# One gap of pad rows after routing, an earlier load for the second head unit, and shared weights loaded inside attention

## The reference, cut to what matters

```python
q, k, v = jnp.split(x @ W_attn.T + b_attn, 3, axis=-1)          # heads: 16 x 16
att = softmax(where(causal, q @ k.T / 4 + rel_bias, -inf))
x = layernorm(x + (att @ v) @ W_proj.T + b_proj)
top1 = argmax(softmax(xf @ gate_w.T))                            # one of two experts
masked = xf[None] * one_hot(top1)                                # the other expert sees zeros
expert_out = relu(masked @ w1 + b1) @ w2 + b2                    # both experts, summed
shared = relu(xf @ sw1 + sb1) @ sw2 + sb2
x = layernorm(x + expert_out.sum(0) + shared)
```

## Time and profile before

| | us |
|---|---|
| median of three executions | 850.62 (843.71 to 852.77) |
| profiled execution, its own time | 847.82 |
| its span in the profile | 846.1 |
| projection, to the first scores of attention | 101.5 |
| attention, 16 units | 101.5 to about 402 |
| PE busy, of the span | 787.3 |
| ACT busy | 547.4 |
| DVE busy | 507.0 |
| POOL busy | 235.2 |

### The profile page before, as it was taken

One profiled execution on the slowest core, in us unless ns is written; L12 is line 12 of the kernel. 1 busy time (PEld: TensorE's weight loads), 2 busy tenths in 40 slices (PEclk: granted clock), 3 DMA queues, 4 the chain that ended last, 5 costly groups with the idle time before them and its releaser, 6 DMA issues.

```text
span 846.1 us, 15471 instructions
## 1 busy us (share of the span) xinstructions
PE 787.3 (93%) x5805; PEld 561.3 (66%) x5805; DVE 507.0 (60%) x1102; ACT 547.4 (65%) x700; POOL 235.2 (28%) x194
## 2 busy tenths in 40 slices
PE   6999879999989989999699999999999999999993
PEld 4887523333433333343588998989899889999893
DVE  3666645667656656766696777775734455545443
ACT  4666578999979979999544555543445545554452
POOL 5224400000200020023253553443334222233332
PEclk9999887999999989999799999999999999999997
DMA  5899899786996998692671211201084344444300
GB/s 203 223 290 287 200 231 193 166 168 109 175 217 114 160 189 167 109 144 71 119 249 57 76 52 58 70 29 49 32 295 153 129 156 163 176 176 159 138 26 29
DMA packets 58375, 122.86 MB, mean 145 GB/s; under 512 B 8211, under 2 KB 35256, under 8 KB 55736
## 3 DMA queue, kind: packets, MB, share of 16 engines
q1 hardware_dynamic: 53496, 109.09, 53.5%
q0 software_dynamic: 4800, 12.73, 4.3%
HBM read 66.27 MB, written 40.98 MB: 127 GB/s over the span
## 4 chain that ended last, share of the span: by engine, by line
PE 74%; DMA 8%; DVE 6%; SPq 4%; ACT 4%; issue 2%; POOLq 0%; POOL 0%; DVEq 0%; ACTq 0%
PE slots L1927 21%; PE slots L1941 11%; PE o_ps L1941 10%; PE o_ps L1152 9%; PE slots L1133 8%; DMA q_second<-guard_d 6%; PE slots L694 6%; ACT probs L1043 3%; PE slots L1335 2%; PE o_ps L655 2%; DVE slots L1100 2%; DMA rsum_d<-rsums 1%; PE slots L1911 1%; ACT probs L1045 1%; PE slots L636 1%
## 5 line engine op out<-in xcount | busy, mean ns | idle before, releaser
L1043 ACT ACTIVATE probs<-slots 128x1024 f32<-128x1024 f32 x252 | 238.3, 1035 | 14.3 <-DVE slots L1100 8.5
L1100 DVE TENSOR_TENSOR slots<-slots,bias_t 128x512 f32<-128x512 f32 (+1 forms) x288 | 160.4, 606 | 97.5 <-PE slots L1133 96.7
L1836 DVE TENSOR_TENSOR h_lo<-h_f,h_hi 128x512 fp32r<-128x512 f32 (+1 forms) x136 | 96.8, 713 | 113.1 <-PE o_ps L1941 70.6
L1152 PE MATMUL o_ps<-probs,v_st 128*32 128x512 f32 (+3 forms) x1664 | 160.2, 487 | 2.1 <-DVE o_sb L1063 0.5
L1666 ACT ACTIVATE h_f<-slots,b_cur 128x512 f32<-128x512 f32 (+1 forms) x72 | 47.9, 665 | 89.0 <-PE slots L1927 88.0
L1666 ACT ACTIVATE h_f<-slots,b_c 128x512 f32<-128x512 f32 x64 | 44.0, 688 | 72.5 <-PE slots L1927 69.1
L1670 ACT ACTIVATE h_hi<-h_f 128x512 fp32r<-128x512 f32 (+1 forms) x136 | 84.3, 620 | 4.3
L1133 PEld LDWEIGHTS slots<-q_second,k_st 50*128 50x128 f32 x416 | 34.4, 193 | 72.4 <-ACT probs L1043 43.9
L1133 PE MATMUL slots<-q_second,k_st 50*128 50x512 f32 (+3 forms) x416 | 68.6, 401 | 13.1 <-DMA q_second<-guard_d 9.2
L1133 PEld LDWEIGHTS slots<-q_first,k_st 50*128 50x128 f32 x416 | 34.7, 188 | 65.6 <-ACT probs L1043 43.5
L1152 PEld LDWEIGHTS o_ps<-probs,v_st 128*32 128x32 f32 x1664 | 40.5, 110 | 54.0 <-issue 32.3
(11 more groups left out here) (227 smaller groups left out, 1745.6 us busy)
## 6 DMA issues: line engine op xcount, KB each, us to landing
qk_d<-parts SPq DMA_DIRECT2D x32, 512.0 KB, 8.3
cur_hi<-experts_hi SPq DMA_DIRECT2D x9, 1024.0 KB, 4.9
cur_lo<-experts_lo SPq DMA_DIRECT2D x9, 1024.0 KB, 6.9
k_st<-qk_d SPq DMA_DIRECT2D x32, 256.0 KB
xs_d<-xs_d SPq DMA_DIRECT2D x8, 528.0 KB, 11.5
xs_sb<-xs_d SPq DMA_DIRECT2D x8, 528.0 KB, 4.9
x_in<-L_attn_x SPq DMA_DIRECT2D x8, 512.0 KB, 8.0
k_st<-qk_d SPq DMA_DIRECT2D x32, 128.0 KB
```

What stands on the lines that cost most here:

```text
L1043: nc.scalar.activation(dst, src, ACT.Exp).then_inc(exped, 1)
L1100: ins = dve.tensor_tensor(tile, tile, bias_t[:, h0:h0 + 2, first:first + w], ALU.add)
L1152: ins = pe.matmul(o_ps[32 * j2:32 * j2 + 2 * D, half, q:q + w], v_st[:, g, j, j2, :], probs[:, (k + j2 // 2) % PBUFS, j2 % 2, col:col + w] ...
L1836: dve.tensor_tensor(h_lo[:, n % 3, 0:w], h_f[:, q % 2, 0:w], h_hi[:, n % 3, 0:w].bitcast(F32), ALU.subtract).then_inc(hl_ok, 1)
```

## The change

It does four things. First, the stacks of unit 1 of batch 0 are loaded in `project_in`: its eight transfers stand behind the eight of unit 0, and ahead of the guard rows of both units and of the stores of tiles 6 and 7. Second, the shared weights are loaded in the body of batches 1 and 2, behind `load_stacks(b + 1, 0)`. Third, `put_pads` is gone with its 18 transfers; in its place `fill_gap` writes the 512 unused rows of each array from `pad_row` when the routing is known: DVE copies `n_first` to an integer `gap_i`, SP loads it in a register, issues two transfers (528 and 512 KB), and waits for them before it loads the first routed rows. Fourth, POOL no longer waits for the pads before its first scatter. The branch on `wide` is changed to match, for both units.

```diff
@@ project_in
             load_parts(sp, *unit_rows(qk_d, 0, 0), k_st[:, 0], q_first, st_ld[0])
+            load_parts(sp, *unit_rows(qk_d, 0, 1), k_st[:, 1], q_second, st_ld[1])
             sp.wait_ge(guard_out, 16)
-            load_guard(sp, guard_d, 0, 0, q_first, st_ld[0])
+            for g, q_st in enumerate((q_first, q_second)):
+                load_guard(sp, guard_d, 0, g, q_st, st_ld[g])
             body(B - 1, True, False)
@@ attend, sync
-            load_stacks(0, 1)
-            sp.wait_ge(ready.norms, TILES)
-
-            for i, src in enumerate((sw1, sw2)):
+            def load_shared(i):
+
+                src = (sw1, sw2)[i]
                 sp.dma_start(shared_raw[:, i].rearrange("p (k c) -> p k c", c=src.shape[1]),
                              src.rearrange("(k p) c -> p k c", p=P)).then_inc(sw_ld, 16)
+
+            sp.wait_ge(ready.norms, TILES)
             for t in range(TPB):
                 sp.wait_ge(ready.stored[t], 16 * 2 * KC * B)
-
-            def put_pads(n):
...
-            sp.wait_ge(ones_ok, 3)
@@
-                pads = range(EXP_TILES * b // (B - 1), EXP_TILES * (b + 1) // (B - 1)) if after else ()
-                for n in pads[0:1]:
-                    put_pads(n)
                 move_unit(b, 0)
                 load_stacks(b, 3)
-                for n in pads[1:2]:
-                    put_pads(n)
                 move_unit(b, 1)
                 if after:
                     load_stacks(b + 1, 0)
-                for n in pads[2:]:
-                    put_pads(n)
+                if 1 <= b <= 2:
+                    load_shared(b - 1)
                 move_unit(b, 2)
@@ feed_forward
+        def fill_gap():
+
+            sp.wait_ge(ready.ones, 3)
+            sp.wait_ge(gap_ok, 1)
+            first = sp.value_load(gap_i[0:1, 0:1], min_val=0, max_val=B * T)
+            for dst, width in ((xs_d, ROW), (base_d, C)):
+                sp.dma_start(dst[bass.ds(first, TT)].rearrange("(k p) c -> p k c", p=P),
+                             pad_row[:, 0:width].unsqueeze(1).to_broadcast([P, NB, width])).then_inc(ready.pads, 16)
+
+        fill_gap()
         sp.wait_ge(route_ok, 2)
@@
         sp.wait_ge(tile.proj_ps, TILES)
+        sp.wait_ge(ready.pads, 32)
         load_rows(0)
@@
                 pool.wait_ge(made, 6)
-                pool.wait_ge(ready.pads, 32 * EXP_TILES)
@@
                 dve.wait_ge(first_ok, 2)
+                dve.tensor_copy(gap_i[:, :], n_first[:, :]).then_inc(gap_ok, 1)
```

More of the change, by code:

```diff
@@ L305, in project_in @@
 def project_in(nc, keep, ready, slots, o_ps, ident, wp_hi, wp_lo, bp_row, v_all, shared_at, y_at, bias_t, wide, neg_guard, guard_fill, qk_d, guard_d, pad_row, rs_at,
-               k_st, v_st, q_first, st_ld, x_tiles, w_attn, b_attn, w_proj, b_proj, rel_emb, buckets):
+               k_st, v_st, q_first, q_second, st_ld, x_tiles, w_attn, b_attn, w_proj, b_proj, rel_emb, buckets):
     HG = H // KC
@@ L730, in project_in, with exact_maxima @@
         return Stage(sync, gpsimd, scalar, vector, tensor)
-def exact_maxima(nc, keep, ready, slots, o_ps, ident, bias_t, wide, qk_d, guard_d, q_first, st_ld, shared_at):
+def exact_maxima(nc, keep, ready, slots, o_ps, ident, bias_t, wide, qk_d, guard_d, q_first, q_second, st_ld, shared_at):
     HG = H // KC
@@ L765, in sync @@
                     sp.wait_ge(ready.stored[t], 16 * 2 * KC * B)
-                sp.wait_ge(st_ld[0], 16 * ST_DMAS)
+                for ld in st_ld:
+                    sp.wait_ge(ld, 16 * ST_DMAS)
                 with sp.Fori(0, B) as b:
@@ L778, in sync @@
                 sp.wait_ge(neg_out, 16 * GUARD * (B + 1))
-                load_guard(sp, guard_d, 0, 0, q_first, neg_out)
-                sp.wait_ge(neg_out, 16 * GUARD * (B + 1) + 32)
+                for g, q_st in enumerate((q_first, q_second)):
+                    load_guard(sp, guard_d, 0, g, q_st, neg_out)
+                sp.wait_ge(neg_out, 16 * GUARD * (B + 1) + 64)
         def vector(dve):
@@ L936, in move_sums @@
                                  ).then_inc(sum_in, 16)
-            load_stacks(0, 1)
-            sp.wait_ge(ready.norms, TILES)
-            for i, src in enumerate((sw1, sw2)):
+            def load_shared(i):
+                src = (sw1, sw2)[i]
                 sp.dma_start(shared_raw[:, i].rearrange("p (k c) -> p k c", c=src.shape[1]),
                              src.rearrange("(k p) c -> p k c", p=P)).then_inc(sw_ld, 16)
+            sp.wait_ge(ready.norms, TILES)
             for t in range(TPB):
                 sp.wait_ge(ready.stored[t], 16 * 2 * KC * B)
-            def put_pads(n):
[L949 to L955, removed]
-                                     pad_row[:, 0:width].unsqueeze(1).to_broadcast([P, NB, width])).then_inc(ready.pads, 16)
-            sp.wait_ge(ones_ok, 3)
             def body(b, before, after):
```

9 lines of the change are left out of this document (5 added, 4 removed).

## The result

The change takes 843.75 us (median of 20 executions, 839.87 to 847.24). The kernel before took 848.00 us on the same chip (20 executions, 842.22 to 853.91). The ratio is 0.9952, with a 95% interval of 0.9933 to 0.9972: 4.1 us faster, or 0.5%. The forecast was 8.3 us less, 842.3 us, with a range of 835 to 850 us. So the time lies in the range, and the gain is half of the forecast.

What follows compares the result with a forecast made beforehand. Mostly TensorE bounds the chain, with ACT setting an undisturbed attention unit's pace and stops at odd units; 7.5 + 0.8 + 0 = 8.3 us off the 850.6 us median gives 842.3 us, range 835 to 850 us.

Steps and rivals of the forecast that it cites:

- Part 1: Pads in attention batches 1 and 2: without them unit 3's load is less late, 7.47 us gained.
- part 2: Early load of unit 1's stacks in batch 0: 6.04 us won, 5.2 us lost at unit 0, net 0.8 us gained.
- signs of being wrong: Unit 0 near 101.5 or after 109; batch 1 or 2 stops over 1.5 us; or L1911 waiting for `xs_sb`.
- the pads were not the cause: Batches 1 and 2: row sums alone make the load late; 3.0 us gained in all, 847.6 us; chance 0.13.
- I take 10 us: nothing else is queued at 96.: Second unit's stacks in batch 0 take 10 us of the DMA engines, so `q_first`'s guard rows land at 106.7.
- slow second load: Batch 0: the second unit's load takes 13 us; 5.3 us gained in all, 845.3 us; chance 0.14.
- I price its own length at no change, and the clock's recovery with it.: Unit 0 of batch 0 starts at half clock either way, so its length was priced at no change.
- The gain at unit 1: Batch 0: the stop at 125.68 and the slow clock behind it go, 6.04 us of ACT's standing still.
- Queue order: Batch 0: guard rows wait behind the second unit's stacks, keeping 0.8 us gained; if they overtook, 6.0 us.
- not held up: Batch 0: guard rows land unhindered, PE starts unit 0 at 101.5; 13.5 us gained in all, 837.1 us; chance 0.14.
- Part 3: Gap fill before the first routed rows: delay priced at 0, with a stop of 0 to 3 us as range.
- fill too late: Gap fill delays the first routed rows, a 6.0 us stop; 2.4 us slower than before, 853.0 us; chance 0.05.

Runs made afterwards that it cites:

- the pads' part with the row sums moved: Changed kernel with unit 1's stacks and shared weights loaded as before, row-sum loads behind unit 3's load: 838.17 us, ratio 0.9920 to the kernel before.
- the pads' part alone: Changed kernel keeping the gap fill and dropped pads, with unit 1's stacks and shared weights loaded as before: 840.94 us, ratio 0.9910 to the kernel before.
- the guard rows first: Changed kernel with unit 0's guard rows issued ahead of unit 1's eight parts: 842.48 us, ratio 0.9929 to the kernel before.

## Why the prediction was half right

The forecast was 8.3 us less, the spans of the two traces differ by 4.3. Part 1 came out 0.7 us under its term, part 2 2.2 us, and the feed-forward part lost 1.2 us where nothing was put. Of the prediction's own signs of being wrong, two came: unit 0 started after 109, at 109.98, and the stop of unit 3 in batch 1 stayed over 1.5 us, at 1.85. `L1911`, now L1910, showed no wait.

**Part 1, the pads: right in mechanism and size.** The term was 7.47 us. The part alone brought 7.6 us by its ratio (4.6 to 10.7) and 7.7 us in its trace, and the trace of the change has 2.59 + 4.86 - 0.64 = 6.8 us. Taking batch 3, which has no pads, as the measure for the others was the right choice; it was not exact (a stop of 1.85 us in batch 1, none in batch 2, 1.34 in batch 3). Behind both stops the granted clock stayed at 1.00 (237 to 245 and 377 to 385 us). The rival that the pads were not the cause falls.

**Part 2, the second unit's stacks: the mechanism right, the price too low.** The term was 6.04 - 5.2 = 0.8 us gained; alone it lost 3.7 us. This is the step that failed. In the pair of traces it can be taken apart: unit 0 starts 8.5 us later, takes 0.7 us less, the stop of 3.24 us goes, and unit 1 takes 18.28 us in place of 147.12 - 125.68 = 21.44, so 3.16 us less. That is 8.45 - 0.7 - 3.24 - 3.16 = 1.35 us lost.
- *"I take 10 us: nothing else is queued at 96."* The guard rows were to land at 106.7. They let PE go only at 109.98, and PE started 8.5 us later than before, not 5.2. This is the term that was mis-sized. The engines moved 126 to 170 GB/s, not the 171 of the first unit all through, and were full to 109, so the second unit took 109 - 96 = 13 us. The only second load in the rows had also taken 13.0 us, and nothing there gave 10. The prediction had this case as the rival "slow second load", at 845.3 us and 0.14: 5.3 us gained, nearer to the measured 4.1 than the forecast.
- *"I price its own length at no change, and the clock's recovery with it."* The clock fell in the longer stop and came back at 120.2, 9 us later than before. This made unit 0 no longer: it took 20.2 us, against 125.68 - 3.24 - 101.5 = 20.9 before.
- The gain at unit 1 was priced at 6.04 us from one execution, and against that execution it is there: 3.24 + 3.16 = 6.4 us. But half of it is the fall of the clock behind the stop. In the pads' part with the row sums moved, the stop was 2.11 us and unit 1 took 143.09 - 124.17 = 18.9 us, so less was to be won. A gain of which half is a fall of the clock is not in every execution.

Against the trace of the pads' part alone the change loses 2.4 us up to unit 2. The rest of the 3.7 us lies between executions, and stays open. That the projection itself ended 2.4 us later in the change's trace (DVE writes `neg_guard` at 103.39, before at 100.94) has no part in the late start, as PE waited for the guard rows to 109.98 in any case.

**Queue order: right.** The guard rows wait for what is queued ahead of them. The change's own trace has PE waiting for them for 7.23 us, and with them first PE started at 101.18, so the rival "not held up" falls. The rule of the Trainium skill, page "DMA: Bandwidth & Descriptors", section "Queues, rings and completion order", that each engine takes its ring in order, fits: issued at 93.10 behind the second unit, the guard rows of `q_first` let PE go only when the engines had finished it. That completion need not be first in, first out didn't help them.

**What the prediction didn't see** is the branch, at which DVE stands 6 us longer under full DMA engines. It hardly bears on the change's own time, as shown, but it took away most of what the guard rows first would have brought.

**Part 3, the gap: right.** The term was 0. PE turned the first routed rows without a stop, and the part alone lost nothing. The rival "fill too late" falls: the fills took 4.9 and 6.0 us, not 17.2 and not over 11. The 1.2 us in the feed-forward part were not in the sum; no experiment isolated them, and they are smaller than the spread of that part from trace to trace. The shared weights, moved at a price of 0, were not moved alone either. The two parts without them add up to the change within 0.2 us, but each part is known only to some 3 us.

## What to carry to other kernels

Before a load is moved ahead of others, look at every small transfer that is then queued behind it: one of two rows can hold the start of a stage as long as megabytes do. Price a load by the nearest load of its kind that the trace shows, here 13 us, and say why if you take less. Where an execution shows several stops of one kind, the one that lacks the suspected cause prices it. What the clock's fall behind a stop costs in one execution need not be there in the next. When one wait is taken away, ask what passed in its shadow: here it was a branch, and with the large load issued behind it DVE's gap was short again.

## What the runs showed of the hardware

- With a branch over code that is not run DVE stood still for 8.2 us while the DMA engines were full, and for 2.3 and 2.2 us when they had a share of 0.50 and 0.51 in the gap (the kernel before, and unit 1 loaded behind the branch). Without the branch the gap was 1.0 us under full engines. SP's issue of a transfer from `guard_fill` also took longer in that stretch, and there the branch had no part: 4.78 us with it, 4.37 without, and 0.48 us in the kernel before. First with the branch, then without:

```profile
104.97 4.78 SPq L441 DMA_DIRECT2D guard_d<-guard_fill  x1
```

```profile
106.06 4.37 SPq L441 DMA_DIRECT2D guard_d<-guard_fill  x1
```

- The same stop of 2.37 or 2.38 us in the projection left the clock at its full level in the kernel before and dropped it in the changed one. First before, then after:

```profile
84.90 0.73 PE L694 MATMUL slots<-xt_hi,wq_hi 128*128 128x512 f32 x2 [2.37 <-DVE xt_lo L527]
85.47 0.62 PE L694 MATMUL slots<-xt_hi,wq_lo 128*128 128x512 f32 x2
```

```profile
85.82 0.85 PE L696 MATMUL slots<-xt_hi,wq_hi 128*128 128x512 f32 x2 [2.38 <-DVE xt_lo L529]
86.47 1.05 PE L696 MATMUL slots<-xt_hi,wq_lo 128*128 128x512 f32 x2
```

  Two matmuls take 1.05 us in place of 0.62. The clock fell so in six of the twelve traces, without a change in the code ahead of it (in the kernel before without its branch it fell, in the pads' part alone it held). DVE writes `neg_guard`, near the end of the projection, at 102.9 to 104.7 us in those six and at 100.6 to 101.5 us in the others. The feed-forward part too differs by up to 6 us between traces. Both are a reason not to read a difference of 2 us from one trace.
